# An earlier mask request, and layer norms that pass through their chain one batch at a time

## The reference

```python
def _ln(x, g, b, eps=1e-05):
    m = jnp.mean(x, axis=-1, keepdims=True)
    v = jnp.mean(jnp.square(x - m), axis=-1, keepdims=True)
    return (x - m) / jnp.sqrt(v + eps) * g + b

def step(t, p):                       # six times
    tn = _ln(t, norm_g, norm_b)
    t = _mha(tn, tn, skv, sq, sow, sob, tgt_mask) + t    # self-attention
    tn = _ln(t, norm_g, norm_b)
    t = _mha(src, tn, ckv, cq, cow, cob, src_mask) + t   # cross-attention
    tn = _ln(t, pg, pb)
    t = t + (jax.nn.relu(tn @ w1 + b1) @ w2 + b2)
    return (t, None)
# _mha: kv = s @ kv_w; q = t @ q_w; softmax(q k^T / 8, masked) v, then @ o_w + o_b
```

## Time and profile before

| | us |
|---|---|
| median of three runs | 2954.28 (2951.63 to 2956.06) |
| profiled execution | 2950.49 |
| its span, first to last instruction | 2948.5 |
| PE busy | 2807.1 (95%) |
| DVE busy | 1713.6 (58%) |
| ACT busy | 1304.0 (44%) |
| POOL busy | 1129.8 (38%) |
| mean granted PE clock | 0.990 |

### The profile page before, as it was taken

How to read it: one execution, slowest core, us unless ns; L and a number is a source line. 1 busy time by engine, 2 the same in 40 slices (tenths; PEclk the granted TensorE clock), 3 DMA queues, 4 the chain that set the end, 5 groups by cost and what they waited for, 6 DMA issues and landing times.

```text
span 2948.5 us, 64849 instructions
## 1 busy us (share of the span) xinstructions
PE 2807.1 (95%) x24616; PEld 2329.9 (79%) x24616; DVE 1713.6 (58%) x6432; ACT 1304.0 (44%) x4273; POOL 1129.8 (38%) x1313
## 2 busy tenths in 40 slices
PE   6878999999999999999999999999999999999999
PEld 4656887887887887887887887888888888888887
DVE  3445664664664664655665665665655655655655
ACT  2224544544544543544544444444444444444444
POOL 2203443443443443444433444433443433333333
PEclk9999999999999999999999999999999999999999
DMA  6205234336334336333335243344352334332330
GB/s 211 93 15 192 85 131 157 85 106 201 85 131 151 90 106 194 86 137 118 109 121 157 104 155 99 117 131 142 118 157 79 129 112 121 117 100 78 110 104 24
DMA packets 178762, 350.32 MB, mean 119 GB/s; under 512 B 17997, under 2 KB 142486, under 8 KB 169110
## 3 DMA queue, kind: packets, MB, share of 16 engines
q1 hardware_dynamic: 168086, 195.18, 22.9%
q0 software_dynamic: 10368, 151.00, 14.1%
HBM read 307.48 MB, written 38.67 MB: 117 GB/s over the span
## 4 chain that ended last, share of the span: by engine, by line
PE 81%; DVE 6%; POOL 5%; DMA 4%; issue 2%; ACT 2%; SPq 0%; DVEq 0%; POOLq 0%; ACTq 0%
PE proj L665 18%; PE sum L986 16%; PE score L665 13%; PE proj L685 7%; PE sum L685 7%; PE sum L665 5%; PE proj L1007 3%; PE score L839 2%; DMA smask<-self_mask 2%; PE sum L863 2%; PE proj L944 2%; PE tr L850 1%; PE tr L944 1%; POOL stage_parts L549 1%; PE proj L657 1%
## 5 line engine op out<-in xcount | busy, mean ns | idle before, releaser
L622 POOL TENSOR_TENSOR prob<-prob,rtotal 128x375 f32<-128x375 f32 x672 | 543.5, 811 | 648.4 <-DVE rtotal L1590 647.4
L1063 ACT ACTIVATE prob<-prob,negmax 128x375 f32<-128x375 f32 (+1 forms) x686 | 418.0, 609 | 439.1 <-DVE negmax L1581 406.7
L986 PE MATMUL sum<-pT,ctx 32*128 32x224 f32 (+1 forms) x4608 | 500.6, 358 | 14.8 <-DVE qcT L1573 14.8
L986 PE MATMUL tr<-pT,ctx 32*128 32x224 f32 (+1 forms) x4608 | 500.6, 358 | 0.0
L986 PEld LDWEIGHTS sum<-pT,ctx 32*128 32x128 f32 (+1 forms) x4608 | 417.9, 185 | 68.1 <-issue 62.6
L1581 DVE CUSTOM_DVE_ANT_0 prob<-score,cbias 128x375 f32<-128x375 f32 x672 | 357.4, 532 | 183.2 <-PE score L665 179.5
L986 PEld LDWEIGHTS tr<-pT,ctx 32*128 32x128 f32 (+1 forms) x4608 | 417.0, 185 | 0.0
L1599 DVE STREAM_TRANSPOSE pT<-prob 128x384 f32<-128x384 f32 x672 | 373.5, 559 | 0.0
L665 PE MATMUL score<-ctx_parts,qc_high 128*128 128x376 f32 x1344 | 368.2, 355 | 0.0
L579 POOL TENSOR_TENSOR prob<-prob,rtotal 112x448 f32<-112x448 f32 x200 | 186.3, 931 | 452.2 <-DVE rtotal L1451 452.2
L1142 ACT ACTIVATE prob<-prob,negmax 112x112 f32<-112x112 f32 x800 | 298.8, 376 | 85.9 <-DVE negmax L1469 85.9
(11 more groups left out here) (240 smaller groups left out, 5249.8 us busy)
## 6 DMA issues: line engine op xcount, KB each, us to landing
w_vq_parts<-sa_v_parts POOLq DMA_DIRECT2D x24, 2048.0 KB, 8.7
w_kf_parts<-sa_k_parts POOLq DMA_DIRECT2D x24, 2048.0 KB, 8.4
w_vq_parts<-sa_q_parts POOLq DMA_DIRECT2D x24, 2048.0 KB, 8.7
w_kf<-ff_w SPq DMA_DIRECT2D x48, 1024.0 KB, 7.0
ctx<-ctx SPq DMA_DIRECT2D x192, 176.0 KB
stage<-sa_kv SPq DMA_DIRECT2D x24, 512.0 KB, 3.8
sa_v_parts<-stage_parts SPq DMA_DIRECT2D x12, 1024.0 KB, 5.5
sa_q_parts<-stage_parts SPq DMA_DIRECT2D x12, 1024.0 KB, 4.8
```

What stands on the lines that cost most here:

```text
L622: pool.tensor_tensor(row, row, rtotal[:, G * SG + i:G * SG + i + 1].broadcast_to([P, S2]), ALU.mult).then_inc(prob_ready, 1)
L986: ins = pe.matmul(bank[:, 0:HT * R], ctx4[keys_of, m // (HALVES // NB), j, :], pT[keys_of, m % 2, :, j * R:(j + 1) * R], start=j == 0, sto ...
L1063: act.activation(o, i, ACT.Exp, bias=negmax[0:rows, col:col + 1], scale=scale, accum_out=total[0:rows, col:col + 1]).then_inc(exp_ready, 1)
```

## The change

There are three edits. SP requests the self mask as the first thing in an iteration. The norms of the decoder signal and wait per batch: `bn_aggr` of each batch has its signal, POOL handles one column at a time (`inverse_deviation`, 112x1), and in the first two norms DVE normalises batch 0 before the residual of batch 1. PE's `normed` waits for each batch and transposes it. Last, the second norm's transposes stand ahead of the first duo's sums on PE, and ACT's scaling ahead of its copy of those sums.

```diff
@@ SP, loop over iterations
                 rounds = rounds_in(it)
+                sp.wait_ge(smask_used, it + 1)
+                load_pair_smask(next_p)
                 if new_layer:
 ...
                 for r in rounds[0:1]:
                     store_parts(r)
                     load_raw(r + 1)
-                sp.wait_ge(smask_used, it + 1)
-                load_pair_smask(next_p)
@@ POOL
+            def inverse_deviation(at):
+                k = at.next("norm")
+                pool.wait_ge(mv_ready, at.at("norm", k + 1))
+                b = slice(k % NB, k % NB + 1)
+                pool.tensor_tensor(veps[:, 0, b], mv2[:, 0, b, 1], eps[:, 0, b], ALU.add).then_inc(pool_step, 1)
+                pool.wait_ge(pool_step, at.at("pool", at.next("pool") + 1))
+                pool.tensor_tensor(rstd2[:, 0, b], veps[:, 0, b], minus_half[:, b], ALU.pow).then_inc(deviation_ready, 1)
 ...
-                    inverse_std(at, 0)
+                    for i in range(NB):
+                        inverse_deviation(at)
                     pool.wait_ge(tn_ready, at.at("tn", NB))
 ...
-                    for g in range(4):
+                    for g in range(3):
                         normalise_group(at, g)
-                    inverse_std(at, 0)
+                    inverse_deviation(at)
+                    normalise_group(at, 3)
+                    inverse_deviation(at)
                     pool.wait_ge(tn_ready, at.at("tn", 2 * NB))
 ...
                     for g in range(4, 7):
                         normalise_group(at, g)
-                    inverse_std(at, 0)
+                    for i in range(NB):
+                        inverse_deviation(at)
                     normalise_group(at, 7)
@@ PE
             def normed(at, n, name, a=tn):
-                pe.wait_ge(tn_ready, at.at("tn", NB * (n + 1)))
-                transposes_of(at, a, name)
+                bank = fill(at, name)
+                for b in range(NB):
+                    pe.wait_ge(tn_ready, at.at("tn", NB * n + b + 1))
+                    for k in range(EK):
+                        ins = pe.transpose(bank[:, k * T2 + b * S:k * T2 + (b + 1) * S], a[:, b, k * P:(k + 1) * P],
+                                           ident[0:S, 0:S])
+                done(ins, name)
 ...
                     self_scores(at, 2)
+                    normed(at, 1, "proj0")
                     self_sums(at, 0)
-                    normed(at, 1, "proj0")
                     self_transposes(at, 2)
@@ ACT
                     self_probabilities(at, 0)
-                    attended(at, 0)
                     act.wait_ge(loaded["small"], (l + 1) * (16 * SMALL))
                     normed(at, tnT, pre, "proj0")
+                    attended(at, 0)
@@ DVE
+            def averages(at, ins, batches):
+                link(at, ins)
+                for b in batches:
+                    dve.bn_aggr(mv2[:, 0, b, :], stats[:, b, :]).then_inc(mv_ready, 1)
 ...
+            def normed(at, a, o=tn, batches=range(NB)):
+                for b in batches:
+                    k = at.next("norm")
+                    dve.wait_ge(mv_ready, at.at("norm", k + 1))
+                    dve.wait_ge(deviation_ready, at.at("norm", k + 1))
                     normalise(o[:, b, :], a, b).then_inc(tn_ready, 1)
 ...
-                                ins = dve.bn_stats(stats[:, b, :], o[:, b, :])
-                        if with_statistics:
-                            variances(at, ins)
+                                averages(at, dve.bn_stats(stats[:, b, :], o[:, b, :]), (b,))
+                                if b == 0 and not between:
+                                    normed(at, o, batches=(0,))
 ...
-                    residual(tw, between=lambda: self_reciprocals(at, 3))
+                    def last_reciprocals_and_first_normed():
+                        self_reciprocals(at, 3)
+                        normed(at, tw, batches=(0,))
+                    residual(tw, between=last_reciprocals_and_first_normed)
                     self_probabilities(at, 1)
-                    normed(at, tw)
+                    normed(at, tw, batches=(1,))
```

More of the change, by code:

```diff
@@ L77, in attention_layers @@
              "tr1": 2 * NU, "sum0": 3 * NU + 3 * NU // 2, "sum1": 3 * NU, "stats": NU, "tn": NU, "resid": 2 * NU, "negmax": 3 * NB * NU,
-             "exp": 3 * NB * NU, "prob": 3 * NB * NU, "rtotal": 0, "turned": 0, "dve": (4 * NB + 2) * NU, "pool": NU, "high": 0, "tn_high": 0}
+             "exp": 3 * NB * NU, "prob": 3 * NB * NU, "rtotal": 0, "turned": 0, "dve": (4 * NB + 2) * NU, "pool": NU, "high": 0, "tn_high": 0, "norm": 0}
     SELF_MASKED = -1.0e30
@@ L321, in attention_layers @@
         tn_ready = sem("tn_ready")
+        mv_ready = sem("mv_ready")
+        deviation_ready = sem("deviation_ready")
         resid_ready = sem("resid_ready")
@@ L582, in _ @@
             at = Place(START)
-            inverse_std(at, 0)
-            inverse_std(at, 0)
+            for i in range(2 * NB):
+                inverse_deviation(at)
             for g in range(SG):
@@ L1304, in normalise, with both_averages @@
                 return dve.tensor_scalar(o, a[:, b, :], mv2[:, u, b, 0:1], rstd2[:, u, b:b + 1], ALU.subtract, ALU.mult)
-            def normed(at, a, o=tn):
-                wait_rstd(at)
-                for b in range(NB):
+            def averages(at, ins, batches):
+                link(at, ins)
+                for b in batches:
+                    dve.bn_aggr(mv2[:, 0, b, :], stats[:, b, :]).then_inc(mv_ready, 1)
+            def both_averages(at, a):
+                for b in range(NB):
+                    ins = dve.bn_stats(stats[:, b, :], a[:, b, :])
+                averages(at, ins, range(NB))
+            def normed(at, a, o=tn, batches=range(NB)):
[3 more added lines that the diff above has]
+                    dve.wait_ge(deviation_ready, at.at("norm", k + 1))
                     normalise(o[:, b, :], a, b).then_inc(tn_ready, 1)
@@ L1411, in _ @@
                         dve.wait_ge(taken["proj1"], at.emptied("proj1", at.n["proj1"]))
-                        statistics(START_PLACE, first)
+                        both_averages(START_PLACE, first)
                     if n == 2 and u == 1:
@@ L1497, in _ @@
             second = t_all[:, NB:2 * NB, :]
-            statistics(at, second)
+            both_averages(at, second)
             self_maxima(at, 2)
@@ L1639, in _ @@
                     self_reciprocals(at, 6)
-                    statistics(at, next_tokens)
+                    both_averages(at, next_tokens)
                     self_reciprocals(at, 7)
@@ L1650, in _ @@
                     attended(at, 3)
-                    assert all(at.n[k] == MAIN[k] for k in ("proj1", "tr1", "sum1", "dve", "stats", "resid"))
+                    assert all(at.n[k] == MAIN[k] for k in ("proj1", "tr1", "sum1", "dve", "resid"))
 _DECODER = ["sa_kv", "sa_q", "sa_ow", "sa_ob", "ca_kv", "ca_q", "ca_ow", "ca_ob", "ff_w1", "ff_b1", "ff_w2", "ff_b2",
```

5 lines of the change are left out of this document (2 added, 3 removed).

## The result

The changed kernel takes 2909.82 us, the median of four runs (2909.01 to 2911.45), against 2955.17 for the kernel before (2951.63 to 2956.94, four runs on the same chip). The ratio is 0.9849, 95% interval 0.9832 to 0.9866. The forecast was 2896 within 2882 to 2930: the direction is right, and so is the mechanism of the larger part, the mask; the norms gave much less than forecast, and the point is 14 us too low. The profiled execution took 2909.43 us, its span is 2907.6 (before 2948.5).

A forecast was written before the change was run, and what follows sets the result against it. PE, busy 95%, was taken as the bound, losing time to waits or a lowered clock. Mask -38, first norm -11.3, second -12.5, third +3.4 gave -58 us: 2892 against the profiled execution, 2896 on the median, range 2882 to 2930.

The forecast's parts named there:

- The step by which all of the excess counted: Iterations 1 to 19 run 38.1 us too long; the early mask request wins all, -38, not only 26 of DVE waits.
- Rival C: Half of the mask's excess stays, from late landing for pair 0 or sbias meeting POOL's cast: 2915 us; chance 0.10.
- rivals A: The forecast itself: POOL's power on one column costs about 0.45 us, giving 2896 us; chance 0.55.
- rival B: POOL's power costs the same for one element as for two, fixed per instruction: -30 in all, 2924 us; chance 0.30.
- x: Cost of POOL's power on 112x1, taken as 0.45 us, the middle between 0.19 and 0.71.
- -11.3 forecast: First norm per batch: 0.64 us won in each of ten iterations, 0.35 in each of fourteen split ones.
- the floor: First norm: PE can't go on before 497.74, when its four transposes are through, so at most 0.64 us counts.
- the step on the residual: First norm, split iterations: DVE waits for POOL's late first power, so the second residual starts 0.31 us late.
- -12.5 forecast: Second norm per batch, transposes ahead of the first duo's sums: first f_1 matmul 0.52 us earlier in each iteration.
- +3.4 forecast: Third norm: POOL does addition and power twice, so PE's last self transposes come 0.14 us later, 24 times.
- rival D: Slower: DVE's in-order queue stands behind POOL in every norm, the third above all: +12 us, 2966; chance 0.03.
- The collision: Third norm: POOL's last group slows one DVE normalise from 0.40 to 1.01 us; forecast to fall on batch 1.

The follow-up runs named there:

- the fastest kernel here: Changed kernel with third norm whole and early, second norm's transposes behind the sums again, one wait before DVE's normalise: 2892.08 us, ratio 0.9794.

## Why the prediction was right, and where its sizes were off

**The mask: as forecast.** The term was -38, the move alone measured -37.8, both between profiled executions. The step by which all of the excess counted and not only DVE's 26.2 us of waits was the right one, since PE's clock came back too: no stretch at a lowered clock stands between 270 and 2900. (An estimate from the rows of the kernel before: 26.3 us of PE's waits for oT, and five stretches of 3.41 us at half the clock, 1.7 us lost in each, make 34.8 of the 38.1.) With the request where the prediction put it, pair 0's mask lands 10.4 to 10.9 us into the iteration (10.9 was forecast) and all others before it begins. Rival C is excluded by that.

One reading under it was wrong. The 15 waits for the mask are not the 15 split iterations: iteration 0 splits and has no wait, and the fifteenth is iteration 19, which splits nothing. Its request stands at 8.35 us, behind the next layer's w_o, and the mask takes 6.88 us to land (1.18 us of wait). It changed nothing in the sum, because the move puts that request first as well.

And part of the nearness to the forecast is luck. The kernel before scatters, 2950.5 to 2961.09 us in 13 runs, and its profiled execution is at the low end; the mask alone gives 2912.11 to 2914.84 in four. By the medians of the two the move is worth 42.8 us. The prediction took its 38 off a median, which is some 5 us too little, and that hides as much of what the norms missed: against the profiled execution its 2892 is 17 too low, not 14. By the time alone rivals A (2896) and B (2924) are equally far from 2910; what decides between them is x.

**The power's cost x: mis-sized.** Taken 0.45, measured 0.557. The middle between the bounds was right in kind and wrong in size: against the 0.71 of 112x2, one column costs 0.15 less, so some 0.40 of each power is fixed and rival B's argument was partly true. By the Trainium skill, "GPSIMD Engine Reference" (section "2. Architecture"), half the vector steps had given the estimate of 0.45; the row says 0.557. With x = 0.557 the prediction's own formulas give -9.9 us for the second norm instead of -12.5 and +8.5 for the third instead of +3.4, where it counts twice in a row. So of 17.5 us that the norms missed (forecast -20.4, they gave -2.9), 7.7 are this one number. In the first norm the formulas would give -7.4, but there another limit binds before x does.

**First norm: -11.3 forecast, -5.4 measured** (c_v starts 0.26 us earlier in an iteration that splits nothing, 0.20 in a split one). The step that failed is the floor: it was read too early. PE was to be held only by its own transposes until 497.74. But it also wants the bank that the v copy empties, and that copy can't start before the values themselves are through. In iteration 3, PE:

```profile
604.89 0.63 PE L680 MATMUL proj<-w_vq_parts,tnT_next_low 128*112 128x512 f32 x2
605.36 0.55 PE L819 MATMUL sum<-ident,qcT 112*128 112x112 f32 x4
606.31 1.19 PE L680 MATMUL proj<-w_vq_parts,tnT_next_high 128*112 128x512 f32 x4 [0.40 <-DVE v L1468]
```

and DVE:

```profile
605.01 0.41 DVE L1322 TENSOR_SCALAR qcT<-tw,mv,rstd 112x256 f32<-112x256 f32 x1 [1.01 <-POOL rstd L583]
605.56 0.69 DVE L1468 COPY v<-proj 112x512 f32<-112x512 f32 x1
```

The values end at 605.52, the copy runs from 605.56 to 606.25, PE goes on at 606.31. However early the normalise, PE stands 0.40 us here. The same distances laid on iteration 2 before, where the values end at 497.34, let PE go on at 498.13 and not at 497.74, instead of 498.38: 0.25 us can be won there and not 0.64, whatever x is, and 0.26 was. In split iterations the step on the residual held: it starts at 493.17, 0.30 us late behind the first normalise (0.31 was forecast), and with it the gain is 0.20.

**Second norm: -12.5 forecast, -6.9 measured.** The first f_1 matmul comes 0.23 us earlier relative to c_v, the f_2 matmul another 0.06. Of the 0.52 forecast for f_1, x takes 0.11, the second wait in front of the normalise 0.07, and the work behind it 0.12: from the second batch's transposes to f_1 it is 2.07 us (572.07 to 574.14) where 1.95 was reckoned, most of it in the two transposes themselves (0.34 until the sums start, not 0.2). The step that failed in kind is that the new order was never priced against the old one. The old one lets the sums cover the wait for the second batch and leaves 0.44 for tnT; the new one covers tnT and leaves 0.65 in front of the second batch's transposes with nothing beside it. The chain per batch alone was enough; the order costs 0.15 to 0.17 an iteration, some 4 us in 24. The cover of 0.1 us for the residual held:

```profile
568.23 0.94 DVE L1322 TENSOR_SCALAR qcT<-tw,mv,rstd 112x256 f32<-112x256 f32 x1 [0.96 <-POOL rstd L583]
569.37 0.42 DVE L1569 TENSOR_TENSOR tw<-proj,tw 112x256 f32<-112x256 f32 x1 [0.20 <-PE proj L700]
```

The normalise is held by POOL's fourth group (0.94 instead of 0.41), and the residual still waits for PE and not for it.

**Third norm: +3.4 forecast, +9.4 measured** (+0.39 an iteration instead of +0.14: x adds 0.21, the second wait in front of the normalise 0.07, and 0.03 came back). DVE:

```profile
585.36 0.41 DVE L1322 TENSOR_SCALAR qcT<-t_all,mv,rstd 112x256 f32<-112x256 f32 x1 [0.49 <-POOL rstd L583]
586.29 0.94 DVE L1322 TENSOR_SCALAR qcT<-t_all,mv,rstd 112x256 f32<-112x256 f32 x1 [0.52 <-POOL rstd L583]
```

POOL:

```profile
584.70 0.55 POOL L583 TENSOR_TENSOR rstd<-veps,minus_half 112x1 f32<-112x1 f32 x1
585.48 0.70 POOL L583 TENSOR_TENSOR rstd<-veps,minus_half 112x1 f32<-112x1 f32 x1
```

The copy that empties tr, for which PE waits, follows at 587.48. The collision stands where it was put, on batch 1: POOL's last group begins at 586.15. Only one normalise is held, so rival D's three holds did not come; a second small one did, which was in no case: the second power takes 0.70 instead of 0.55 while DVE normalises batch 0 beside it. This is so in each of the 24 iterations.

**What was in no term.** The second wait in front of each normalise cost 0.15 us in an iteration that splits nothing, 0.07 each in the second and the third norm, and 0.24 in a split one; iterations 1 to 19 are 4.9 us shorter (2084.3 against 2089.2) and 20 to 22 0.4. This and the 4 us of the order don't add up in full: with the old order the first f_1 matmul stands 16.10 us behind c_v with two waits and with one. In the fastest kernel here the norms win 2090.9 - 2076.1 = 14.8 us in iterations 1 to 19 over the mask move alone, and 0.74 in each of 20 to 22, some 17 in all (the two ran on different chips). So most of the 20.4 forecast could be had, but with the third norm whole and early, the old order in the second and one wait.

## What to carry to other kernels

A load's lateness is read from what it stands behind in its queue. Here one wait for a store's landing ahead of a small load cost 38 us, and it moved 26 us of visible waits and a lowered clock at once. Splitting a chain over engines by batches paid here where the batches' inputs come apart in time (the first two norms) and lost where they come together (the third), since each engine's fixed cost is then paid twice in series. When a chain gets shorter, look for what holds the waiting engine next: in the first norm it was a copy that empties its bank, and it left 0.25 us to win and not 0.64. And scatter can point at a late transfer: the two kernels with the late mask spread over 10.6 us (13 runs) and 12.2 (10 runs), those with the mask early over at most 4.9, in four runs each. That the mask makes the scatter was not tried by itself. An entry on the list of waits is not a gain to be had: ask which work is queued behind the instruction that would now wait in its place.

## What the runs showed of the hardware

- Of two semaphore waits in front of one DVE instruction, one is an instruction of its own on DVE's sequencer (148 of 21 ns, line 1341). Here it was the one written second, for POOL, which also came last. It shows as 0.11 us from POOL's end to DVE's start instead of 0.03 to 0.04. Whether the other order of the two waits would avoid it was not tried.
- A power on 112x1 takes 0.557 us on POOL, on 112x2 0.71; an addition takes 0.19 and 0.20. One column more costs 0.15 of the power and nearly nothing of the addition.
- In the kernel before, PE stood for oT for 2.14 to 2.95 us in iterations 8, 9, 12, 16 and 18, and each had a stretch of 3.41 us at 1.2 GHz beside it, which began between 0.2 us before and 1.6 us behind its end. In the ten other split iterations it stood for up to 1.71 us, and none had one. No sharp limit follows: with the norms alone a stand of 2.08 us (iteration 2) had such a stretch behind it, and one of 2.13 (iteration 9) had none.
- A normalise (112x256) on DVE takes 0.94 us beside POOL's 0.93 us group, and 0.41 alone. The delay, 0.53, is again not the whole of POOL's instruction.
- A power on 112x1 takes 0.70 us beside a normalise on DVE instead of 0.55, in 24 of 24 cases.
